# One inter-block product set per tile, and a tile's blocks ordered by half and batch, in the encoder's causal linear attention

## The reference

```python
q, k, v = x @ Wq + bq, x @ Wk + bk, x @ Wv + bv       # heads of 16
q, k = elu(q) + 1, elu(k) + 1
A = einsum('bnihd,bnjhd->bnhij', q, k) * tril(ones)    # inside a chunk
intra = einsum('bnhij,bnjhm->bnihm', A, v)
inter = einsum('bnihd,bnhdm->bnihm', q, KV)            # KV: sum of k v^T over the chunks before
out = (intra + inter) / (den + EPS)                    # den: the same sums with v = 1
x = layer_norm(x + out @ Wo + bo, g1, be1)
x = layer_norm(x + gelu(x @ W1 + b1) @ W2 + b2, g2, be2)
```

## Time and profile before

| | us |
|---|---|
| median of 3 runs | 1510.44 (1509.41 to 1511.5) |
| profiled execution | 1508.9 |
| its span, first to last instruction | 1507.2 |
| TensorE busy | 1466.3 (97%) |
| VectorE busy | 1236.6 (82%) |
| GpSimd busy | 1023.9 (68%) |
| ScalarE busy | 981.4 (65%) |

### The profile page before, as it was taken

One profiled execution on the slowest core, in us unless ns is written; L12 is line 12 of the kernel. 1 busy time (PEld: TensorE's weight loads), 2 busy tenths in 40 slices (PEclk: granted clock), 3 DMA queues, 4 the chain that ended last, 5 costly groups with the idle time before them and its releaser, 6 DMA issues. The chain is left out here.

```text
span 1507.2 us, 38734 instructions
## 1 busy us (share of the span) xinstructions
PE 1466.3 (97%) x16021; PEld 1169.7 (78%) x16021; DVE 1236.6 (82%) x2082; ACT 981.4 (65%) x1604; POOL 1023.9 (68%) x970
## 2 busy tenths in 40 slices
PE   9999999999999999999999999999999899998898
PEld 7788888888888888888888888888877566665434
DVE  7888898888988889888898888988885799988547
ACT  4667657676576765667666676575644788887444
POOL 4656667766677666776667766677568699986534
PEclk9999999999999999999999999999999899999999
DMA  5210002100121001210012100010106445543001
GB/s 138 72 41 8 19 26 72 42 14 19 26 72 41 16 18 27 71 43 14 17 26 72 43 15 16 26 44 18 36 15 150 148 155 164 161 147 87 1 1 56
DMA packets 91766, 82.00 MB, mean 54 GB/s; under 512 B 17652, under 2 KB 79816, under 8 KB 91592
## 3 DMA queue, kind: packets, MB, share of 16 engines
q1 hardware_dynamic: 91456, 79.49, 18.2%
q10 hardware_dynamic: 136, 0.04, 0.0%
HBM read 50.79 MB, written 14.68 MB: 43 GB/s over the span
## 5 line engine op out<-in xcount | busy, mean ns | idle before, releaser
L880 POOL TENSOR_TENSOR e_h_lo<-e_h_f,e_h_hi 128x512 fp32r<-128x512 f32 x192 | 260.6, 1365 | 199.4 <-ACT e_h_hi L652 196.4
L651 ACT ACTIVATE e_h_f<-e_pr,e_h_bias 128x512 f32<-128x512 f32 x192 | 131.9, 687 | 217.2 <-PE e_pr L194 212.7
L1001 DVE TENSOR_TENSOR e_am<-e_sc,c_amask 128x1024 f32<-128x1024 f32 x184 | 216.5, 1217 | 47.1 <-PE e_sc L453 47.1
L2022 DVE TENSOR_REDUCE x_mx<-x_psS 128x4 f32<-128x1024 f32 x128 | 154.5, 1211 | 30.2 <-PE x_psS L1606 30.2
L192 PE MATMUL e_tr<-e_W_hi,e_h_hi 128*128 128x256 f32 x576 | 165.4, 287 | 1.0 <-POOL e_h_lo L880 1.0
L192 PE MATMUL e_pr<-e_yT_hi,e_W_hi 128*128 128x512 f32 x384 | 165.9, 432 | 0.1
L193 PE MATMUL e_tr<-e_W_lo,e_h_hi 128*128 128x256 f32 x576 | 162.9, 283 | 0.0
L194 PE MATMUL e_tr<-e_W_hi,e_h_lo 128*128 128x256 f32 x576 | 162.9, 283 | 0.0
L1774 ACT ACTIVATE x_ex<-x_psT 128x1024 f32<-128x1024 f32 x128 | 131.0, 1023 | 45.5 <-PE x_psT L1628 43.3
L193 PE MATMUL e_pr<-e_yT_lo,e_W_hi 128*128 128x512 f32 x384 | 151.0, 393 | 0.0
L194 PE MATMUL e_pr<-e_yT_hi,e_W_lo 128*128 128x512 f32 x384 | 149.7, 390 | 0.0
(11 more groups left out here) (316 smaller groups left out, 4427.2 us busy)
## 6 DMA issues: line engine op xcount, KB each, us to landing
e_raw_m<-in_L_attn_W_dram SPq DMA_DIRECT2D x12, 1024.0 KB, 5.5
x_qs<-query_rows SPq DMA_DIRECT2D x48, 256.0 KB
e_x_raw<-e_x_blocks SPq DMA_DIRECT2D x352, 32.0 KB, 1.9
x_ks<-key_rows SPq DMA_DIRECT2D x48, 128.0 KB, 2.8
query_rows<-x_q_hi SPq DMA_DIRECT2D x16, 256.0 KB, 2.3
query_rows<-x_q_lo SPq DMA_DIRECT2D x16, 256.0 KB, 2.3
x_ctok<-in_ctx_dram SPq DMA_DIRECT2D x8, 256.0 KB, 2.9
x_xo<-in_x_dram SPq DMA_DIRECT2D x8, 256.0 KB, 2.8
```

Source lines behind the costliest of these rows:

```text
L651: act.activation(h_f[:, m % HR, :], ps_pr[m % 2][:, :], ACT.Gelu, bias=h_bias[:, l * FC + m:l * FC + m + 1])
L880: pool.tensor_tensor(h_lo[:, m, :], h_f[:, m % HR, :], h_hi[:, m, :].bitcast(F32), ALU.subtract).then_inc(h_lo_done, 1)
L1001: dve.tensor_tensor(am[:, s % 2, c, :, :, :], ps_sc[:, :, c * 2 * P:(c + 1) * 2 * P].rearrange("p r (h n) -> p r h n", n=P), amask[:, :].u ...
L2022: dve.tensor_reduce(mx[:, N % 2, :, 0:HG].rearrange("p i (a h) -> p h a i", a=2)[:, pair], ps_s[pair][:, :, :].rearrange("p a (i j) -> p a ...
```

## The change

- A tile's blocks are now ordered half 0 of both batches, then half 1 of both batches. X is loaded so, `key_values` reads blocks 2 and 3, and the stage behind the encoder finds its rows by `encoded(e, s)`. The last tile's normalisation takes blocks in the order 0, 2, 1, 3.
- `attend_all` handles both blocks that have an inter term (now 0 and 1) in one set of 16 instructions on 32x64 tiles: a head pair's two 32-wide blocks of `kv` are one 64-wide stationary operand. Row group a goes to bank a // 2, columns (a % 2) * 64.
- The output of one block is spread over both banks of `ps_tr2`, a half of the heads each, and a bank holds two blocks. One VectorE transpose of 128x1024 turns both blocks, `to_tokens(pair)`; `attend(2)` waits for the first of them.
- The features come out in another order (c, row group, i), so Wo's rows are loaded in that order by eight DMAs.

```diff
+            def load_wo(l):
+                rows = dram["Wo"][l, :, :].rearrange("(c i g d) n -> c g i d n", c=KC, i=2, d=DH)
+                for c in range(KC):
+                    for g in range(NR):
+                        sp.dma_start(raw_a[g * RH:(g + 1) * RH, names_a.index("Wo"), c], rows[c, g]).then_inc(raw_o_loaded, 16)
...
+            def load_x(i, done):
+                for h in range(2):
+                    sp.dma_start(X[:, SB * i + 2 * h:SB * i + 2 * h + 2], xv[i, h]).then_inc(done, 16)
...
-                def out_block(s, g, rows):
-                    return ps_tr[s % 2][rows, :].rearrange("p (c j i n) -> p c i j n", c=KC, j=NR, n=RH)[:, g // 2, g % 2]
+                def out_block(s, c, i, rows):
+                    first = s % 2 * D + c * P
+                    return ps_tr2[rows, i, first:first + P]
 
                 def attend(s):
-                    attend_all(s)
+                    if s == 0:
+                        attend_all()
+                    if s == 2:
+                        pe.wait_ge(ob_done, 2 * t + 1)
                     attend_masked(s)
...
-                    if s > 1:
-                        pe.wait_ge(ob_done, SB * t + s - 1)
...
-                    if s % 2 == 0:
-                        pe.wait_ge(kv_done, 2 * t + s // 2 + 1)
-                        for g in range(4):
+                    pe.wait_ge(kv_done, 2 * t + 2)
+                    for b in range(2):
+                        for c in range(KC):
                             for a in range(NR):
-                                rows = slice(a * RH, (a + 1) * RH)
-                                pe.matmul(out_block(s, g, rows), kv[rows, s // 2, g // 2, g % 2, :], qkT[rows, g // 2, blk(s)],
-                                          start=(g == 0), stop=False, skip_group_check=True)
+                                rows, cols = slice(a * RH, (a + 1) * RH), slice(a % 2 * 2 * HP, (a % 2 + 1) * 2 * HP)
+                                pe.matmul(out_block(b, c, a // 2, cols), kv[rows, b, c, :, :].rearrange("p h d -> p (h d)"),
+                                          qkT[rows, c, blk(b)], start=(b == 0 and c == 0), stop=False, skip_group_check=True)
...
-                def to_tokens(s):
-                    dve.wait_ge(out_full, SB * t + s + 1)
-                    if s >= 2:
+                def to_tokens(pair):
+                    dve.wait_ge(out_full, SB * t + 2 * pair + 2)
+                    if pair == 1:
                         dve.wait_ge(norm_step, NORM * (2 * t) + 3)
-                    dve.transpose(ob[:, s % 2, :, :].rearrange("p g n -> p (g n)"), ps_tr[s % 2][:, :]).then_inc(ob_done, 1)
+                    dve.transpose(ob[:, :, :, :].rearrange("p b (k i) n -> p (b k) i n", i=2),
+                                  ps_tr2[:, :, :].rearrange("p i (k n) -> p k i n", n=RH)).then_inc(ob_done, 1)
...
                     mask(1)
+                    mask(2)
                     to_tokens(0)
-                    mask(2)
-                    to_tokens(1)
                     if q >= 0:
                         denominators(0)
                     mask(3)
...
                 if attn and q >= 0:
                     divide(0)
-                    to_tokens(2)
                     to_features(0)
                 if following and q >= 0:
                     x_lo(t + 1, 1)
                 if attn and q >= 0:
-                    to_tokens(3)
+                    to_tokens(1)
                     attn_lo(0)
```

More of the change, by code:

```diff
@@ L380, in step @@
                         for c in range(KC):
-                            mm = pe.transpose(turned_bank(u)[:, blk(b * KC + c)], qkT[:, KC + c, blk(2 * b + 1)], ident[:, :])
+                            mm = pe.transpose(turned_bank(u)[:, blk(b * KC + c)], qkT[:, KC + c, blk(2 + b)], ident[:, :])
                     mm.then_inc(ktr_full, 1)
@@ L392, in key_values @@
                                 mm = pe.matmul(kv_bank(t, b)[rows, c * 2 * HX:(c + 1) * 2 * HX], ktok[:, b, c, rows],
-                                               vx[:, 2 * b + 1, c * HC + 2 * r:c * HC + 2 * r + 2, 0:HX], start=True, stop=True,
+                                               vx[:, 2 + b, c * HC + 2 * r:c * HC + 2 * r + 2, 0:HX], start=True, stop=True,
                                                skip_group_check=True)
@@ L474, in attend_all @@
                         pe.wait_ge(yT_lo_done, 2 * u + 2)
-                    if s % 2 == 0:
-                        pe.wait_ge(kv_done, 2 * t + s // 2 + 1)
-                        for g in range(4):
+                    pe.wait_ge(kv_done, 2 * t + 2)
+                    for b in range(2):
+                        for c in range(KC):
                             for a in range(NR):
-                                rows = slice(a * RH, (a + 1) * RH)
-                                pe.matmul(out_block(s, g, rows), kv[rows, s // 2, g // 2, g % 2, :], qkT[rows, g // 2, blk(s)],
-                                          start=(g == 0), stop=False, skip_group_check=True)
+                                rows, cols = slice(a * RH, (a + 1) * RH), slice(a % 2 * 2 * HP, (a % 2 + 1) * 2 * HP)
+                                pe.matmul(out_block(b, c, a // 2, cols), kv[rows, b, c, :, :].rearrange("p h d -> p (h d)"),
+                                          qkT[rows, c, blk(b)], start=(b == 0 and c == 0), stop=False, skip_group_check=True)
                 def attend_masked(s):
-                    for g in range(4):
-                        pe.wait_ge(am_done, 2 * (SB * t + s) + (g // 2 if q >= 0 else 1) + 1)
-                        for a in range(NR):
-                            mm = pe.matmul(out_block(s, g, slice(a * RH, (a + 1) * RH)), vx[:, s, g // 2 * HC + 2 * a + g % 2, :],
-                                           weighted(t, s, g // 2, a, g % 2),
-                                           start=(s % 2 == 1 and g == 0), stop=(g == 3), skip_group_check=True)
+                    for c in range(KC):
+                        pe.wait_ge(am_done, 2 * (SB * t + s) + (c if q >= 0 else 1) + 1)
+                        for i in range(2):
+                            for g in range(NR):
+                                a, p = 2 * i + g // 2, g % 2
+                                mm = pe.matmul(out_block(s, c, i, slice(g * RH, (g + 1) * RH)), vx[:, s, c * HC + 2 * a + p, :],
+                                               weighted(t, s, c, a, p),
+                                               start=(s == 2 and c == 0), stop=(c == KC - 1), skip_group_check=True)
                     mm.then_inc(out_full, 1)
@@ L767, in _ @@
             steps(step)
-            cross.items({N: last_normed(s) for s, N in enumerate(LAST_NORMED)})
+            cross.items({N: last_normed(i) for i, N in enumerate(LAST_NORMED)})
         @block.gpsimd
@@ L1783, in encoder_norm @@
             act.wait_ge(ln_step[1], LS * e)
-            applied(0, e, lambda s: xw[:, s, :], lambda s: X[:, e * QB + s, :], rows)
+            applied(0, e, lambda s: xw[:, s, :], lambda s: X[:, encoded(e, s), :], rows)
         def x1_norm(e, rows):
```

63 lines of the change are left out of this document (33 added, 30 removed).

## The result

| | before | after |
|---|---|---|
| median, same chip | 1509.93 us (1509.01 to 1511.5, 4 runs) | 1521.08 us (1519.22 to 1523.94, 4 runs) |
| profiled execution, its span | 1508.9, 1507.2 us | 1523.94, 1522.2 us |
| granted TensorE clock over the span | 0.996 | 0.993 |

A forecast was written before the change was run, and what follows sets the result against it. It took Wo pair 2 to be bound by two chains, TensorE's and VectorE's up to attn_lo(1). Terms +10.7, -0.9 and +1.0 gave +10.8 us on 1508.9, 1519.7; the median, 1.5 above, 1521 us; range 1503 to 1529.

The forecast's parts named there:

- ordinary tiles: The 16 tiles without W2 pieces: Wo pair 2 starts 0.67 us later in each, +10.7 us in all.
- tile 23 and behind: Last tile's different pattern and the stage behind the encoder: 0, with tile 23 within 0.7 us.
- Step 1: Inter-block products: one set of 16 at block 0 takes 1.00 us, and 1.00 us leaves block 2.
- The rival of 2 us: 32x64 tiles do not go four together: 1.0 us added ahead of scores(2) in 23 tiles, 1544 us; chance 0.08.
- Step 2: VectorE's transposes to tokens: four of 0.71 us become two of 1.25 us, saving 0.3 us in all.
- Step 3: masked(2) newly waits for the first transpose: 0.2 us lost of 1.0 gained, later products 0.80 us earlier.
- Step 4: VectorE up to features(0): it starts at 591.89 instead of 592.61 in the sample tile.
- Step 5: At attn_lo(0): h_lo(5) now comes first by 0.26 us, so Wo pair 2 starts 0.67 us later.
- Step 6: Five tiles with W2 pieces, first of a layer: Wo pair 2 0.79 us earlier or 0.45 later; middle -0.17.
- Step 7: Beginning: one more X issue before Wq, Wk, Wv, +0.45; wider transpose before mask(3) in the first tile, +0.5.

The follow-up runs named there:

- e8: Changed kernel with each 32x64 inter-block instruction issued as two on 32x32 tiles, 32 at block 0: 1522.3 us.
- e1: Changed kernel with attn_lo(0) put ahead of the second transpose to tokens on VectorE: 1502.14 us.
- e2: Changed kernel with one wait added, GpSimd's h_lo(5) waiting for attn_lo(0): 1495.49 us.
- e7: Kernel before with attn_lo(0) put ahead of the fourth transpose to tokens on VectorE: 1507.85 us.
- e9: Kernel before with one wait added, GpSimd's h_lo(5) waiting for attn_lo(0): 1505.25 us.
- e4: Changed kernel with the second halves of X's first two tiles issued by ScalarE and Wo's DMAs behind W1's: 1518.88 us.
- e3: Kernel before with only the loads split, X in two DMAs a tile and Wo in eight: 1511.27 us.
- e12: Changed kernel with attn_lo(0) before the second transpose, GpSimd waiting for it before h_lo(5) and its W2 piece, X's second halves on ScalarE, Wo behind W1: 1494.17 us.
- e10: Changed kernel with the set of 16 inter-block products issued a second time, ahead of masked(2), some output wrong: 1540.05 us.

## Why the prediction was right, point by point

The forecast was 1521 us for the median, and 1521.08 was measured; the profiled execution was put at 1519.7 and took 1523.9. The mechanism of the loss was right: the order at `attn_lo(0)` turned, by about the lead that was forecast. That the sum met the median to 0.1 us is luck. Against the profiled execution its terms were off by +1.7 us (ordinary tiles), -3.0 (W2 tiles), +4.5 (the beginning) and +1.0 (tile 23 and behind), +4.2 together. The times of the prediction are moved by 10.09 us to the sample tile of the kernel after (589.67 against 579.58 at the set).

- **Step 1**, the set: 1.00 us taken, 1.03 measured. The rival of 2 us is refuted: two row groups write to one bank here, each to its own 64 partitions, and the set took no longer; in e8 two row groups with two column tiles each did so, in 1.09 us for 32. The Trainium skill (TensorEngine Tiling, "Restrictions and Gotchas") says that different row tiles cannot access one PSUM bank at the same time. The trace differs for row tiles that write different partitions, with the 1.03 us.
- **Step 2**, the transpose: 1.25 taken, 1.24 measured.
- **Step 3**, masked(2): the view of waits gives 7.6 us in 24 waits of the weight loads for the first transpose, 0.3 each; forecast 0.2. masked(2) starts at 597.89, forecast 597.88.
- **Step 4**, features(0): forecast 601.98, measured 602.02.
- **Step 5**, the order: `h_lo(5)` forecast 604.63, measured 604.69; `attn_lo(0)` 604.89 against 604.88; it ends at 606.53 (606.46); `attn_lo(1)` starts at 611.04 (610.94). The lead of `h_lo(5)` was 0.19 us, not 0.26, and the loss 0.78 us a tile on the average, not 0.67: 1.7 us over 16 tiles. The missing 0.1 us builds up along the chain: 0.04 at features(0), 0.07 at the end of `attn_lo(0)`, 0.10 at `attn_lo(1)`. Two more signs: VectorE waited 1.85 us for scores ahead of mask(2) (forecast 1.8), and the last Wq product started 1.09 us before Wo pair 2 where such products follow each other in 0.23, so TensorE was free for 0.86 us (forecast 0.9; the profile, which counts the end of the last product, shows 0.70). e1 and e2 change the order by two different means and give 19 and 26 us back; the same edits in the kernel before, e7 and e9, give 1 (within the noise) and 3.
- **Step 6**, W2 tiles: -0.17 taken between -0.79 and +0.45; -0.77 measured. The forecast was right that it was a toss-up: `attn_lo(0)` came up 0.02 us before `h_lo(5)`, and the price of that case (-0.79) was right too. A middle between two outcomes of a race is a value that no tile takes. This term was 3.0 us too slow.
- **Step 7**, the beginning: +1.0 taken, +5.5 in the profiled execution. With the clock full e4 and e3 show 0.9 and 0.4 at tile 1, so +1.0 was near; the clock falls were not foreseen. The path to the first products was undersized: they start 1.36 us later than before, not 0.45, because ScalarE gets Wq 1.7 us later (at 6.73 instead of 5.03) though it is issued 0.5 later. The kernel before, then the kernel after:

```profile
8.15 0.48 PE L192 MATMUL e_pr<-e_xT_hi,e_Wq_hi 128*128 128x512 f32 x1
...
9.51 0.47 PE L192 MATMUL e_pr<-e_xT_hi,e_Wq_hi 128*128 128x512 f32 x1 [2.07 <-DVE e_qk_bias L1097]
```

The three further DMAs of X stand behind W1 and not ahead of it, as step 7 has them; W1 was still issued later than its 9.7, at 11.36, since the eight issues for Wo took 5.87 us. The median has some of the clock's loss: the four executions of the kernel after had mean clocks of 0.992 to 0.996, and the one at 0.996 took 1519.2 us.
- **Tile 23 and the stage behind**: 0 taken, -0.8 and +1.8 measured. What makes the stage behind vary between 390.9 and 393.7 us in these kernels I have not settled; it is short where tile 23 is long and the other way round in some of them (e1, e12), but not in e7.

What I had wrong was the sentence that TensorE's work between scores(2) and Wo pair 2 gives nothing unless VectorE's chain gets shorter *too*, read as if the two were apart. Steps 4 and 5 already had VectorE's `x_lo(1)` earlier through gelu 4; I did not see that this is the whole coupling, and built e10's theory against it. The balance for an ordinary tile: the wide transposes and the wait, with the order that they turned, cost 1.68 us (before to e10), the removed set gives 0.90 back (e10 to after), and mending the order gives 1.52 (after to e1). With the order mended the set's saving comes through, as e1 and e12 show.

Not tried: the changed kernel with `x_hi(1)` ahead of gelu 4 and no other edit, and extra work ahead of scores(2).
